# A third dense layer's shared tiles in front, the queries of a unit loaded ahead of its keys, and seven PSUM banks for the first keys of the sigmoid attention

## The reference

```
q = (norm(x) @ Wq.T) * 16**-0.5; k = ctx @ Wk.T; v = ctx @ Wv.T          # 16 heads of 16
o = sigmoid(q k^T) @ v                                                  # layer 2, "sigmoid attention"
x = x + o @ Wo.T

h = norm(x)                                                             # layer 2, "third dense layer"
shared = swiglu(h @ w_shared_in) @ w_shared_out                         # swiglu(a, b) = silu(a) * b
hid    = swiglu(h @ w1_shared)
routed = sum over 8 experts e of gate[:, e] * (hid @ w2[e])             # two of eight gates are not zero
x = x + shared + routed
```

## Time and profile before

| | |
|---|---|
| three runs | 2664.27, 2667.30 and 2671.64 us, median 2667.3 us |
| the profiled execution | 2666.42 us, of which the span of the trace is 2664.6 us |
| TensorE | 2524.6 us busy, 95% of the span, in 18464 matmuls |
| VectorE, ScalarE, GpSimd | 61%, 58% and 14% of the span |
| mean granted clock of TensorE | 0.969 of full speed |

### The profile page before, as it was taken

One profiled execution on the slowest core, in us unless ns is written; L12 is line 12 of the kernel. 1 busy time (PEld: TensorE's weight loads), 2 busy tenths in 40 slices (PEclk: granted clock), 3 DMA queues, 4 the chain that ended last, 5 costly groups with the idle time before them and its releaser, 6 DMA issues.

```text
span 2664.6 us, 46476 instructions
## 1 busy us (share of the span) xinstructions
PE 2524.6 (95%) x18464; PEld 1257.2 (47%) x18464; DVE 1631.1 (61%) x2991; ACT 1544.1 (58%) x2621; POOL 362.5 (14%) x351
## 2 busy tenths in 40 slices
PE   7999999999899889999899999989989999999987
PEld 2434344343377668886233333268733443434433
DVE  5878788879287675442112221057587788888855
ACT  1777777777601221111787978931237777777773
POOL 3020200200003402220011010012212002010001
PEclk7999999999899999999999999999979999999998
DMA  5523334332200011002754646110043343334300
GB/s 123 75 33 43 63 42 72 37 39 26 79 26 16 1 44 28 1 1 62 103 69 68 87 54 71 48 53 1 13 62 63 42 72 42 35 63 47 42 1 32
DMA packets 68636, 125.13 MB, mean 47 GB/s; under 512 B 20979, under 2 KB 45630, under 8 KB 64966
## 3 DMA queue, kind: packets, MB, share of 16 engines
q1 hardware_dynamic: 67270, 119.73, 29.3%
q10 hardware_dynamic: 1152, 2.44, 0.4%
HBM read 41.59 MB, written 2.10 MB: 16 GB/s over the span
## 4 chain that ended last, share of the span: by engine, by line
PE 81%; DVE 9%; ACT 4%; issue 2%; SPq 2%; POOL 1%; ACTq 1%; DMA 1%; POOLq 0%; DVEq 0%
PE psum L203 38%; PE psum L749 20%; PE psum L214 13%; PE psum L2120 6%; DVE mpart L938 4%; ACT probs L816 3%; PE psum L309 1%; SPq L1063 1%; PE psum L759 0%; PE psum L2113 0%; DVE x L1408 0%; ACTq L1064 0%; DMA qst<-qp_lo 0%; PE psum L768 0%; ACTq L1063 0%
## 5 line engine op out<-in xcount | busy, mean ns | idle before, releaser
L816 ACT ACTIVATE probs<-psum 128x512 f32<-128x512 f32 (+3 forms) x2080 | 1268.1, 686 | 286.7 <-PE psum L203 278.6
L938 DVE TENSOR_REDUCE mpart<-psum 128x2 f32<-128x804 f32 x1024 | 970.9, 990 | 220.1 <-PE psum L203 206.2
L749 PE MATMUL psum<-probs,vt 128*17 128x512 f32 (+1 forms) x4992 | 650.3, 599 | 3.9 <-ACT probs L816 3.2
L203 PE MATMUL psum<-qst,kst 64*128 64x512 f32 (+3 forms) x2496 | 600.4, 438 | 19.7 <-ACT probs L816 7.8
L203 PE MATMUL psum<-kst,qst 62*128 62x402 f32 x2048 | 467.6, 412 | 26.3 <-DVE mpart L938 25.3
L203 PEld LDWEIGHTS psum<-qst,kst 64*128 64x128 f32 (+3 forms) x2496 | 282.2, 182 | 379.9 <-issue 203.5
L203 PEld LDWEIGHTS psum<-kst,qst 62*128 62x128 f32 x2048 | 225.9, 192 | 305.7 <-DVE mpart L938 194.5
L749 PEld LDWEIGHTS psum<-probs,vt 128*17 128x17 f32 (+1 forms) x4992 | 92.2, 96 | 212.9 <-issue 177.5
L214 PE MATMUL psum<-wv,ctxT 128*32 128x256 f32 (+1 forms) x2448 | 170.9, 398 | 3.3 <-ACT vt L839 3.1
L214 PE MATMUL psum<-ctxT,wk 128*32 128x512 f32 (+1 forms) x1536 | 146.4, 507 | 8.9 <-DMA ctxT<-in_ctxT 8.1
L2168 ACT ACTIVATE inner<-psum 128x512 f32<-128x512 f32 x32 | 19.2, 599 | 199.2 <-PE psum L2120 199.2
(11 more groups left out here) (339 smaller groups left out, 2609.9 us busy)
## 6 DMA issues: line engine op xcount, KB each, us to landing
kst<-kp_hi SPq DMA_DIRECT2D x144, 200.1 KB, 5.9
ctxT<-in_ctxT SPq DMA_DIRECT2D x36, 512.0 KB, 5.0
kst<-kp_lo SPq DMA_DIRECT2D x72, 200.1 KB, 5.4
qst<-qp_hi SPq DMA_DIRECT2D x144, 64.0 KB, 4.5
kst<-kp_hi SPq DMA_DIRECT2D x84, 100.1 KB, 2.9
qst<-qp_lo SPq DMA_DIRECT2D x72, 64.0 KB, 5.1
kst<-kp_lo SPq DMA_DIRECT2D x42, 100.1 KB, 3.0
stage<-in_L_ffn_W SPq DMA_DIRECT2D x16, 256.0 KB, 4.1
```

The lines of the kernel that those rows point to most:

```text
L203: last = e.matmul(dst, lhsT, rhs, start=i == 0, stop=i == len(pairs) - 1)
L749: t = e.matmul(c.bank(self.acc)[32 * h:32 * h + VW, :], self.vt[0:kn, kc, self.head(g, h), :], p[0:kn, h % self.wide, :], start=kc == 0, s ...
L816: e.activation(self.probs[n % slots][0:kn, :, :], c.psum[0:kn, k:k + self.wide, :], ACT.Exp if softmax else ACT.Sigmoid, scale=DH ** -0.5) ...
L938: e.tensor_reduce(self.mpart[:, :, p * (SEQ // P) + qt, i], c.psum[:, k:k + 2, 0:MAX_WIDTH], AX.X, ALU.max).then_inc(c.drained(k), 1)
```

## The change

1. In the third dense layer a batch's four `f2_shared` steps now stand ahead of its sixteen `f2_routed` steps. `f2_shared` waits only for the shared hidden steps, the first `f2_routed` of a batch for the routed ones. The last three `f2_split` steps stand behind batch 0's last hidden step.
2. In all three attentions a unit's load issues its six query DMAs first and then its six key DMAs, and the queries have their own semaphores (`queries_in0` to `queries_in2`). The first `query` step of the next batch waits for the halves and the queries alone, and its first `keys` step for the keys. What needs a unit whole waits for both. The halves keep one semaphore each, in the new order.
3. The prelude of the sigmoid attention goes round seven banks, 3, 4, 5, 7, 0, 1, 2, instead of four.

```
-            maxima, prelude, between = None, Ring(3, 4, 5, 7), misc
+            maxima, prelude, between = None, Ring(3, 4, 5, 7, 0, 1, 2), misc
...
+    def queries_in(self, u):
         of_slot = [v for v in range(UNITS) if v % GROUPS and v % 3 == u % 3]
-        return self.c.sem(f"unit_in{u % 3}"), 16 * LOADS * (len(of_slot) * self.past + of_slot.index(u) + 1)
+        return self.c.sem(f"queries_in{u % 3}"), 16 * LOADS // 2 * (len(of_slot) * self.past + of_slot.index(u) + 1)
...
+    def wait_unit(self, e, u, p):
+        if u % GROUPS == 0:
+            e.wait_ge(*self.half_in(u, p))
+        else:
+            e.wait_ge(*self.queries_in(u))
+            e.wait_ge(*self.keys_in(u))
...
             for p in range(HALVES):
-                e.wait_ge(*self.unit_in(GROUPS * (b - 1), p))
+                e.wait_ge(*self.half_in(GROUPS * (b - 1), p))
             for u in range(GROUPS * (b - 1) + 1, GROUPS * b):
-                e.wait_ge(*self.unit_in(u, 0))
+                e.wait_ge(*self.queries_in(u))
+        elif b and step[0] == "keys" and step[3:] == (0, 0):
+            for u in range(GROUPS * (b - 1) + 1, GROUPS * b):
+                e.wait_ge(*self.keys_in(u))
...
                 for j in range(2):
-                    self.load_parts(e, u, slice(0, HALVES), j, c.sem(f"unit_in{u % 3}"))
+                    self.load_queries(e, u, slice(0, HALVES), j, c.sem(f"queries_in{u % 3}"))
+                for j in range(2):
+                    self.load_keys(e, u, slice(0, HALVES), j, c.sem(f"unit_in{u % 3}"))
...
-        ring, placed = Ring(*range(8)), [(at, ("f2_split", f, j)) for j, at in enumerate((-0.95, 0.05, 0.11, 0.17, 0.235))]
+        ring, placed = Ring(*range(8)), [(at, ("f2_split", f, j)) for j, at in enumerate((-0.95, 0.05, 0.235, 0.24, 0.245))]
...
-            main = []
-            for t in range(4 * g, 4 * g + 4):
-                main += [("f2_shared", f, t)] + [("f2_routed", f, t, e2) for e2 in range(E2 // 2)]
+            tiles = range(4 * g, 4 * g + 4)
+            main = [("f2_shared", f, t) for t in tiles] + [("f2_routed", f, t, e2) for t in tiles for e2 in range(E2 // 2)]
...
-                self.wait_hidden(e, g)
+                self.wait_hidden(e, g, 0)
                 self.wait_pair(e, "wso")
...
+                if t % 4 == e2 == 0:
+                    self.wait_hidden(e, g, 1)
                 self.wait_pair(e, "w2", e2)
```

More of the change, by code:

```diff
@@ L639, in wait_weights, with half_in, keys_in @@
         e.wait_ge(self.c.sem(f"{self.tag}_weights_in"), 16 * (6 if self.softmax else 2))
[L641 to L645, removed]
+    def half_in(self, u, p):
+        return self.c.sem(f"half_in{p}"), 16 * LOADS * (BATCH * self.past + u // GROUPS + 1)
+    def queries_in(self, u):
         of_slot = [v for v in range(UNITS) if v % GROUPS and v % 3 == u % 3]
-        return self.c.sem(f"unit_in{u % 3}"), 16 * LOADS * (len(of_slot) * self.past + of_slot.index(u) + 1)
+        return self.c.sem(f"queries_in{u % 3}"), 16 * LOADS // 2 * (len(of_slot) * self.past + of_slot.index(u) + 1)
+    def keys_in(self, u):
+        of_slot = [v for v in range(UNITS) if v % GROUPS and v % 3 == u % 3]
+        return self.c.sem(f"unit_in{u % 3}"), 16 * LOADS // 2 * (len(of_slot) * self.past + of_slot.index(u) + 1)
+    def wait_unit(self, e, u, p):
[4 more added lines that the diff above has]
+            e.wait_ge(*self.keys_in(u))
     def last_scores(self, u):
@@ L720, in tensor @@
                 if kc == 0:
-                    e.wait_ge(*self.unit_in(u, h0 // 2))
+                    self.wait_unit(e, u, h0 // 2)
                     if softmax:
@@ L1054, in wait_place, with part_places, load_queries, load_keys @@
             e.wait_ge(self.c.sem(f"ones{u}"), 2 * (0, 6).index(self.f) + 2)
[L1056 to L1064, removed]
+    def part_places(self, u, j):
+        head = slice(32 * (u % GROUPS) + DH * j, 32 * (u % GROUPS) + DH * j + DH)
+        return head, [slice(64 * j + DH * i, 64 * j + DH * i + DH) for i in range(len(K_PART))]
+    def load_queries(self, e, u, halves, j, sem):
+        head, places = self.part_places(u, j)
+        for rows, part in zip(places, Q_PART):
+            q = (self.qp.hi, self.qp.lo)[part].bitcast(F32)
+            e.dma_start(self.qst[u % 3].bitcast(F32)[rows, halves, :], q[head, halves, :]).then_inc(sem, 16)
+    def load_keys(self, e, u, halves, j, sem):
+        head, places = self.part_places(u, j)
+        for rows, part in zip(places, K_PART):
+            k = (self.kp.hi, self.kp.lo)[part].bitcast(F32)
+            e.dma_start(self.kst[u % 3].bitcast(F32)[rows, halves, :], k[head, halves, :]).then_inc(sem, 16)
     def load_half(self, e, u, p, heads):
@@ L1070, in load_half @@
         for j in heads:
-            self.load_parts(e, u, slice(p, p + 1), j, self.c.sem(f"half_in{p}"))
+            for load in self.load_queries, self.load_keys:
+                load(e, u, slice(p, p + 1), j, self.c.sem(f"half_in{p}"))
     def sync(self, e):
@@ L2404, in wait_pair, with wait_hidden @@
         e.wait_ge(self.c.sem("f2_lo"), KC * {"wsi": 1, "w1": 2, "wso": 3, "w2": 4 + e2}[name])
-    def wait_hidden(self, e, g):
-        e.wait_ge(self.c.sem("f2_hid_lo"), self.c.nth["f2_hidden", self.f, g, 1, KC - 1])
+    def wait_hidden(self, e, g, which):
+        e.wait_ge(self.c.sem("f2_hid_lo"), self.c.nth["f2_hidden", self.f, g, which, KC - 1])
     def rows_read(self, g):
@@ L2522, in vector @@
                 e.tensor_tensor(c.x[:, t, :], c.x[:, t, :], c.bank(k)[:, 0:DM], ALU.add).then_inc(c.drained(k), 1)
-                self.added = c.drained(k), v
             elif kind == "f2_routed":
@@ L2528, in vector @@
                     e.wait_ge(c.sem("gates_weighed"), c.nth["f2_weigh", f, t // 4])
+                if e2 == 0:
+                    k0, v0 = c.at(("f2_shared", f, t))
+                    self.added = c.drained(k0), v0
                 e.wait_ge(c.filled(k), v)
@@ L2636, in share @@
         self.left = ("values", attention.f, BATCH - 1, LAST_KC)
-        self.loaded = attention.unit_in(UNITS - 1, 0)
+        self.attention = attention
         self.early = [place[:, i * SEQ:(i + 1) * SEQ] for i in range(2)] + [
@@ L2748, in scalar_step @@
             if g == 0:
-                e.wait_ge(*self.loaded)
+                self.attention.wait_unit(e, UNITS - 1, 0)
             e.wait_ge(c.filled(k), v)
```

4 lines of the change are left out of this document (2 added, 2 removed).

## The result

The changed kernel took 2641.99 us (median of 6 runs, 2637.78 to 2646.32) against 2668.95 us for the kernel before, a ratio of 0.9904 with a 95% interval of 0.9892 to 0.9917. A second comparison of the same kernel (experiment 7) gave 0.9930, interval 0.9913 to 0.9947, which is 18.7 us. The traces say how much of this the change brought, and where. The profiled execution took 2643.33 us, its span is 2641.5 us, its mean granted clock 0.972 (before: 2666.42, 2664.6 and 0.969).

A forecast was written before the change was run, and what follows sets the result against it. TensorE, busy 89.72 of 90 us inside the sigmoid attention, was taken to bound the kernel, so its stalls count directly. Gains 7.05 + 2.7 + 7.7 = 17.4 us gave a median of 2649.8 us, range 2643.5 to 2658.

The forecast's parts named there:

- The queries ahead of the keys: Sigmoid attention, batch 1's second query step: queries land earlier, removing a 5.33 us stall and 1.72 of slow clock; gain 7.05.
- the first rival: Sigmoid attention: queries land no earlier, DVE waits as before, 7.05 us are missing, 2656.9; chance 0.12.
- The seven banks: Sigmoid prelude: queries need no drained bank, so the second half's loads and the second scores come 2.7 us earlier.
- with the same 8.7 us from first issue to last landing: Prelude's second half: load time assumed unchanged, so scores start at 1267.5, gain 2.7 us.
- The third rival: Preludes: small query transfers leave DMA engines idle, each half may land 0.5 us later; 1.5 us, 2651.3; chance 0.07.
- bound of 5.7: Prelude's largest possible gain, where TensorE itself is the limit: second scores at 1264.5 instead of 1270.21.
- The third dense layer: Opening: shared products start right behind the logits, removing 5.72 us of standing still and 2.0 of half clock; gain 7.7.
- the second rival: Dense layer: the wait comes back, for splits or the last `hidden_lo`; 2 to 4 us missing, about 2653; chance 0.12.
- in the other batches ... TensorE did not wait for them; the same work in another order gives nothing there: Dense layer's later batches: hidden steps are made a quarter batch ahead, so the new order gains nothing.
- What else is added: New load order in the softmax attentions and 168 TensorE rows waiting for query semaphores: taken as 0, between 0 and 8.4 us.
- the fourth rival: TensorE's 168 added waits are not passed for free: 0.104 us each takes back all gain, 0.2 gives 2683; chance 0.03.
- The sum: Whole kernel: 7.05 + 2.7 + 7.7 = 17.4 us less, 2649.8 as a median.

The follow-up runs named there:

- experiment 7: The changed kernel measured once more against the kernel before; ratio 0.9930, 18.7 us.
- experiment 4: The changed kernel with queries still loaded first but counted on the keys' semaphore; ratio 0.9952 to the kernel before, 12.8 us.
- experiment 6: The changed kernel with w2 splits again between hidden steps, then instead with shared tiles waiting for all four hidden steps; ratios 0.9932 and 0.9923 to the kernel before.
- experiment 5: The changed kernel with shared tiles in front only in batch 0 of the dense layer; ratio 0.9929 to the kernel before.
- experiment 9: The kernel before, unchanged, run once more for a second trace; 2669.79 us.
- experiment 8: The changed kernel with nine prelude value blocks instead of seven, those with other banks, or SP's unit 1 held back; ratios 0.9906, 0.9905, 0.9911.
- dense_only: The kernel before with only the dense layer's part of the change (order, moved splits, two waits); ratio 0.9965, 9.3 us.

## Why the prediction was right in direction and too small

**The queries ahead of the keys** (7.05, measured 7.96). The mechanism held: DVE released by TensorE at 1305.32, no wait, the key step filled without one. The time of the landing was reckoned wrongly, from bytes at 133 GB/s beginning near 1303.1: SP issued the six query loads from 1297.29 to 1300.97, each landed 2.9 to 3.9 us behind its issue, and so all had by about 1304.3, not 1306.1. The step that failed is the size of the clock's part: I counted the query step (3.64 - 1.92), but the lower clock lasted into the scores and values behind it, 2.6 us in all (by stretch, before; the changed kernel has 1.00 in the same place):

```profile
1316.85:1321.90 5.05, 5.05 (x24) 1.25 (x28) 1.29 (x2) 0.58 (x1) 1.27 (x1) 0.50 0.02 5
```

The order alone, without its semaphore, would have ended on the side of the first rival (experiment 4).

**The seven banks** (2.7, measured 3.6). The half's loads start at 1251.39 and 1258.57, forecast 1251.4 and 1258.7, and the banks alone bring 2.7. The step that failed is "with the same 8.7 us from first issue to last landing": with the queries in front it is 1266.60 - 1258.57 = 8.0 (7.8 to 8.4 in the eight traces with this order and seven value blocks, 9.4 in the two with nine, 8.6 to 8.9 in the four with the old order). The third rival had this effect with the wrong sign. The Trainium skill, "DMA: Bandwidth & Descriptors", HWDGE ordering, has each DMA engine take descriptors in the order of its ring; the queries' early landing agrees, but it does not say what the order does to the last landing. The prediction's bound of 5.7 does not come out of its own terms: 1258.7 + 5 x 0.93 + 0.5 is 1263.85, not 1264.5, a gain of 6.4; the lower end of the range rests on it.

**The third dense layer** (7.7, measured 7.8 + 2.6). The opening went as forecast, at the full clock, and without a gap; the second rival, priced at 2 to 4 us, is what comes back, at 3.9 or 4.7, if one of two edits is undone (experiment 6). The step that failed is "in the other batches ... TensorE did not wait for them; the same work in another order gives nothing there". I looked for waits for hidden steps and passed over the 1.93 us for `hrow`, which hangs on DVE's queue. DVE's rows, before and after:

```profile
1856.64 0.72 DVE L361 TENSOR_SCALAR hrow<-x,meanvar,rstd 128x256 f32<-128x256 f32 x2
```

```profile
1833.16 0.73 DVE L361 TENSOR_SCALAR hrow<-x,meanvar,rstd 128x256 f32<-128x256 f32 x2
```

With the new order DVE makes it 16.4 us behind the first turn of rows (1833.16 - 1816.74), with the old order 18.7 (1856.64 - 1837.94). This is the largest term that was missing: 2.6 us at a place where the prediction put nothing, and experiment 5 shows that it is the order in the later batches.

**What else is added** at nothing: right for the waits. The 90 us inside the attention are equally full and the stretch from the scores to the query step takes 36.64 us in both, and the stretches with the softmax attentions are not longer, so the fourth rival is out. Not forecast was the 1.6 us of lower clock late in the attention, which no wait of that length announces; experiment 9 does not show that the change is what removes it.

**The sum.** 17.4 + 0.9 + 0.9 + 0.1 + 2.6 + 1.8 (the column from the key step to the logits) = 23.7, the 23.8 us of the traces; without the last term, which the experiments do not tie to the change, it is 22. The 23.8 us lie within the first comparison's interval (22.2 to 28.8 us) and 0.6 above the second's (14.1 to 23.2). That the first comparison gives 1.8 us more is less than what the stretches ahead and behind vary by; it was not explained further. From the median of 2667.3 us 23.8 us less is 2643.5, the lower end of the range itself. That the first median fell below it and the second, 2646.88, above is luck; that the sum was 6 us short is not. About 8 of the 23.8 us are clock: 2.6 behind the query step, 2.1 in the dense opening, 1.7 behind `hrow`, 1.6 late in the attention. The Trainium skill, "TensorE: Matmul & The Clock Gate", Part 1, advises to take the warm-up as under 1% of a typical span and not to fit a count of slow matmuls. Here the rows stand above that figure: TensorE's busy time times what its granted clock lacks of 1, added up in steps of 1 us over the span, is about 70 us before and 62 us after (an estimate from the table by stretch), 2.6% and 2.3% of the span. The 8 us of this change are only 0.3% of it, but a third of the gain.

## What to carry to other kernels

Price a stall of TensorE with what follows it, read from the granted clock behind it: behind the waits of 5.33, 5.72 and 1.93 us that an edit removed or shortened came a stretch at half the clock, worth some 40 to 90% of the wait, while behind the 2.59 us that stay in the prelude came none. When order changes in a whole layer, look at every wait of the layer for every releaser, not only at the one that the edit names. And judge edits worth a few us by cutting the traces at the same events: between the two traces of one kernel the stretches repeat to 0.05 us (changed) and 0.43 us (before), where medians of six runs differ by 5. But look at the granted clock in each of them first, because a piece of the lower clock that moves is worth 1.5 us.

## What the runs showed of the hardware that was not expected

Waits as short as 1.93 and 2.31 us were followed by 3.4 us at a granted clock of 0.50 (experiments 5 and 6), while one of 0.93 us in the changed kernel was not. The length alone does not decide it, for longer ones were not followed by it either: 2.59 us in the changed prelude, and 2.56 and 2.37 us with nine value blocks (experiment 8). The stretch behind the 2.59 us:

```profile
1257.87:1261.27 3.40, 3.40 (x60) 1.87 (x64) 2.19 (x6) 0.00 (x0) 0.00 (x0) 1.00 0.23 47
```

In both traces of before the clock fell behind two waits of 0.65 and 0.41 us at the same place, and in no other trace with the same waits, not even that of dense_only, which has the same program there. The same loads with the queries in front had all landed, counted from their first issue, 17.25 us later in a whole unit (17.41 to 18.11 with the old order) and 7.8 to 8.4 us later in a half with seven value blocks (8.6 to 8.9). And the first stretch, in which the products are the same, took between 1234.75 and 1244.56 us.
